# A linear-attention layer and a mixture of experts in one kernel: bo by a product, k turned from its 16-bit halves, x loaded once, another order between attention and experts

## The reference

```
x = x + attention(layernorm(x))
x = x + experts(layernorm(x))

attention: q = elu(x Wq + bq) + 1, k = elu(x Wk + bk) + 1, v = x Wv + bv, 16 heads of 16
           s += k_i v_i^T ; z += k_i ; out_i = (q_i s) / (q_i z + 1e-6)   (causal, per head)
           result = out Wo + bo
experts:   logits = x router_w^T (8 experts); top 2, softmax of the two logits
           y_e = gelu(x w1_e^T + b1_e) w2_e^T + b2_e   (256 -> 512 -> 256)
           out = sum of the two y_e, each times its probability
```

## Time and profile before

| | us |
|---|---|
| median of 3 runs | 1067.27 |
| lowest, highest | 1064.74, 1071.63 |
| the profiled execution | 1070.12 |
| its span, first to last instruction | 1068.0 |

### The profile page before, as it was taken

How to read it: one execution, slowest core, us unless ns; L and a number is a source line. 1 busy time by engine, 2 the same in 40 slices (tenths; PEclk the granted TensorE clock), 3 DMA queues, 4 the chain that set the end, 5 groups by cost and what they waited for, 6 DMA issues and landing times.

```text
span 1068.0 us, 31902 instructions
## 1 busy us (share of the span) xinstructions
PE 941.2 (88%) x10010; PEld 771.1 (72%) x10011; DVE 835.4 (78%) x2220; ACT 657.2 (62%) x1248; POOL 670.5 (63%) x580
## 2 busy tenths in 40 slices
PE   6789889988898898899888925899999999999995
PEld 3467667766776676677667723678999999999994
DVE  5779999999999999999998775456666666666663
ACT  8667776777677767767775332445555555555552
POOL 2226587787778777877878452356656656555665
PEclk9899999999999999999999856999999999999998
DMA  5916956546655664566455282355555565555554
GB/s 156 214 58 169 256 145 169 149 138 172 159 123 157 160 174 117 157 170 144 140 154 141 87 313 73 62 81 84 99 93 90 94 98 87 93 98 90 89 98 49
DMA packets 127242, 138.84 MB, mean 130 GB/s; under 512 B 12400, under 2 KB 120304, under 8 KB 126512
## 3 DMA queue, kind: packets, MB, share of 16 engines
q1 hardware_dynamic: 100288, 101.45, 38.1%
q0 software_dynamic: 25680, 35.01, 17.9%
q10 hardware_dynamic: 1184, 1.18, 0.4%
HBM read 71.08 MB, written 66.53 MB: 129 GB/s over the span
## 4 chain that ended last, share of the span: by engine, by line
PE 42%; DVE 35%; issue 8%; DMA 6%; ACT 3%; POOL 3%; SPq 1%; POOLq 0%; DVEq 0%; ACTq 0%
PE pF L488 9%; DVE ahl L1132 8%; PE pS L488 8%; PE pU L488 7%; PE pA L488 4%; DVE xn L1145 4%; PE pO L488 4%; DMA out<-yt,to_token 3%; DVE xn L1233 2%; PE pO L594 2%; DVE pd L1216 2%; DVE st L1111 2%; DVE w1s L1252 2%; ACT ahl L875 2%; DVE v L1192 2%
## 5 line engine op out<-in xcount | busy, mean ns | idle before, releaser
L1680 POOL DMA_INDIRECT out<-yt,to_token x135 | 218.1, 1615 | 178.5 <-DVE yt L1528 90.8
L875 ACT ACTIVATE ahl<-pS 128x512 f16<-128x512 f32 x240 | 141.0, 599 | 82.5 <-PE pS L573 80.9
L1132 DVE SCALAR_TENSOR_TENSOR ahl<-pS,ahl 128x512 f16<-128x512 f32 x240 | 160.8, 680 | 19.8 <-ACT ahl L875 19.4
L1581 POOL DMA_INDIRECT expert_in<-xn,cur x128 | 129.1, 1009 | 35.1 <-issue 33.4
L570 PE MATMUL pS<-cbs 128*128 128x512 bf16 x240 | 92.8, 387 | 23.8 <-DVE ahl L1132 19.9
L1055 ACT ACTIVATE g<-pS,b1s 128x256 f32<-128x256 f32 (+1 forms) x140 | 57.3, 462 | 87.9 <-PE pS L488 87.9
L1494 DVE TENSOR_TENSOR ghl<-g,ghl 128x1024 f16<-128x1024 f32 (+1 forms) x68 | 83.0, 1220 | 20.9 <-ACT ghl L1080 20.9
L488 PE MATMUL pS<-gT,w1s 128*128 128x256 f16 (+1 forms) x840 | 96.4, 271 | 1.0 <-DVE gT L1489 0.9
L488 PE MATMUL pF<-w2s,ghl 128*128 x816 | 95.1, 273 | 2.0 <-issue 1.1
L1539 POOL TENSOR_TENSOR rs<-ve,cfs 128x4 f32<-128x4 f32 x31 | 32.2, 1040 | 102.3 <-DVE ve L1102 102.3
L488 PE MATMUL pF<-xT,was 128*128 128x512 f16 x384 | 93.0, 379 | 3.1 <-DVE xT L1137 2.5
(11 more groups left out here) (193 smaller groups left out, 2293.0 us busy)
## 6 DMA issues: line engine op xcount, KB each, us to landing
xg<-expert_in SPq DMA_DIRECT2D x64, 260.0 KB, 3.1
qk_parts<-qkhl SPq DMA_DIRECT2D x32, 512.0 KB, 2.9
qst<-qk_parts SPq DMA_DIRECT2D x96, 128.0 KB
kst<-qk_parts SPq DMA_DIRECT2D x48, 256.0 KB
xs<-x SPq DMA_DIRECT2D x16, 512.0 KB, 5.4
xr<-x SPq DMA_DIRECT2D x16, 512.0 KB, 4.9
out<-x SPq DMA_DIRECT2D x16, 512.0 KB, 3.2
expert_in<-pads SPq DMA_DIRECT2D x16, 260.0 KB, 3.9
```

What stands on the lines that cost most here:

```text
L875: nc.scalar.activation(ahl[:, b % 2, 0, n * 4 * C:(n + 1) * 4 * C], score_bank(fr, n)[:], ACT.Relu).then_inc(sc_hi, 1)
L1132: V.scalar_tensor_tensor(ahl[:, b % 2, 1, cols], score_bank(fr, n)[:], 0.0, ahl[:, b % 2, 0, cols], ALU.max, ALU.subtract).then_inc(sc_lo, 1)
L1581: G.indirect_dma_start(xg_dram, bass.IndirectOffsetOnAxis(ap=cur[:, qp, 2 * b + t:2 * b + t + 1], axis=0), xn2[:, qp, b], None).then_inc(s ...
L1680: G.indirect_dma_start(out, bass.IndirectOffsetOnAxis(ap=to_token[:, c % 2, s:s + 1], axis=0), yt[:, c % 2, s], None, compute_op=ALU.add). ...
```

## The change

- **bo.** `add_bo`, `xr` and its load are gone. `boh` holds bo x 16 / 64 in 16 bits, its high half in 64 rows and its low half in 64 rows; a product of a matrix of ones (128 rows) with it opens each `out_project`. The residual reads `xs`, which now has three buffers.
- **k's state.** `k_rows` turns the two 16-bit halves of k (16 transposes, into 16-bit PSUM), `kn_rows` copies both, and the state is three 16-bit products per block against the halves of v.
- **Queue of SP.** k is sent ahead of q's loads in every step. The load of the next x comes behind the store of x1.
- **Routing.** `pd` at L1216 is gone: ACT makes the exponential from the two top logits in four small activations. The last operation of `row_data` and the count become reductions. `ixf` and `pos` lie in PSUM.
- **Order.** The third and fourth `norm2_apply` and the second are moved apart; `w1_high` and `w1_low` come later in the step.
- **Between the parts.** The table is worked out for 128 lanes at once in narrow operations and turned by six transposes. Idle products of PE are put in three places (12, 24 and 8). The padding blocks go out from ACT's queue, 128 rows for seven lists and 256 for the last, and ACT then runs one small Gelu. Step 14's slots are found earlier. Four full tiles (`PRE`) come ahead of the split tiles; where expert 0 has 1024 rows or more after step 14, their loads do not wait for the last step's scatters nor for the padding. `w2_low` is spread.

```diff
+PRE = 4
+LEAD = PRE + SPLIT
...
 (SP)
+                    if c >= 2:
+                        sp.wait_ge(xn_done, 4 * (i - 2) + 4)
+                    sp.wait_ge(ln1_st, 4 * i + 4)
+                    sp.dma_start(xs[:, (c + 1) % XB], x_steps[bass.ds(i + 1, 1)]...).then_inc(x_in, 16)
-                    sp.dma_start(xr[:, par], x_steps[bass.ds(i, 1)]...).then_inc(xr_in, 16)
-                    if lead:
-                        send(0, q_out)
-                        send(1, k_out)
+                    send(0, q_out)
+                    send(1, k_out)
                     for t, sent in enumerate((q_out, k_out)):
-                        if not lead:
-                            send(t, sent)
                         sp.wait_ge(sent, 16 * i + 16)
...
+            sp.wait_ge(ready_set, 2)
+            sp.wait_ge(lists_ready, 1)
+            odd_steps = sp.value_load(ready_i[0:1, 0:1], ...)
+            rows_ready = sp.value_load(ready_i[0:1, 1:2], ...)
             sp.wait_ge(tab, TAB)
...
                 if c == 0:
+                    sp.wait_ge(lists_ready, rows_ready)
+                    sp.wait_ge(pads_out, 16 * (E + 1))
+                    sp.wait_ge(scat_out[0], 128 * STEPS // 2)
+                    sp.wait_ge(scat_out[1], odd_steps)
+                if c == PRE:
+                    sp.wait_ge(scat_out[1], 128 * STEPS // 2)
                     sp.wait_ge(tail_out, 16 * E)
 (PE)
+                    for a in range(2):
+                        for b in (2 * n, 2 * n + 1):
+                            for k in range(KC):
+                                mm = nc.tensor.transpose(k_turned[:, a, c0:c0 + P], qkhl[:, 1, a * KC + k, b * C:(b + 1) * C], ident_half)
...
-                        mm = nc.tensor.matmul(pU[...], kn[:, b, k * P:(k + 1) * P], v[:, sp_, b, ...], start=True, stop=True)
+                        mm = split3(pU[...], lambda a, _: kn[:, a, b, k * P:(k + 1) * P], lambda a, _: vhl[:, sp_, a, b, ...], 1)
...
+                    nc.tensor.matmul(pA[:, D:2 * D], chs[0:2 * BR, H_ONES:H_ONES + P], boh[:], start=True, stop=False)
+                    split3(pA[:, D:2 * D], ..., KC, go_on=True).then_inc(wo_ps, 1)
...
                 if c == STEPS + 1:
                     out_project(r, 3)
+                    idle_products(12)
                     for b in range(B):
                         route_transpose(b)
...
+            idle_products(24)
+            pe.wait_ge(tab, TAB_SUMS)
+            (six transposes: experts_wide twice into pA, to_turn columns 1 and 0 into pA, 2 and 3 into pU)
+            idle_products(8)
             pe.wait_ge(tab, TAB)
 (ACT)
-            nc.scalar.activation(kn[:, 2 * n:2 * n + 2]..., pU[:], ACT.Copy)
+            nc.scalar.activation(kn[:, :, 2 * n:2 * n + 2]..., k_turned, ACT.Copy)
+                def top_probability():
+                    act.wait_ge(rt, RT * q + 2)
+                    for b in range(B):
+                        nc.scalar.activation(one_exp[:, b, 1:2], mx[:, b, 0:1], ACT.Exp, bias=mx[:, b, 1:2], scale=-1.0)
...
             for n in range(2, W2Q):
                 w2_high(n)
+            act.wait_ge(tail_done, 1)
+            for e in range(E):
+                row = act.value_load(tails_i[0:1, e:e + 1], ...)
+                act.dma_start(xg_dram[bass.ds(row, P)], pads[:, 0]).then_inc(tail_out, 16)   (256 rows for the last)
+            act.wait_ge(lists_ready, 1)
+            act.wait_ge(tail_out, 16 * E)
+            act.sem_inc(lists_ready, 1)
+            nc.scalar.activation(warm[:], one_exp[:, 0, 0:1], ACT.Gelu)
 (DVE)
-                    V.scalar_tensor_tensor(pd[:, 0], mx[:, :, 1], 1.0, mx[:, :, 0], ALU.mult, ALU.subtract)
-                    V.tensor_tensor(cnt[:], oh[:, :, 0], oh[:, :, 1], ALU.add).then_inc(cnt_done, 1)
+                        V.tensor_reduce(cnt[:], oh[:].rearrange("p b t e -> p b e t"), AX.X, ALU.add).then_inc(cnt_done, 1)
-                    V.scalar_tensor_tensor(xn2[:, qp, :, PROB2], pd[:, 2], 1.0, one_exp[:, :, 1], ALU.mult, ALU.mult)
+                    V.tensor_reduce(xn2[:, qp, :, PROB2], one_exp[:, :, 1:3], AX.X, ALU.mult)
...
-                        norm2_apply(1)      (was beside norm2_apply(0); now behind score_lo(1, 2))
-                        norm2_apply(3)      (was beside norm2_apply(2); now behind score_lo(2, 0))
-                if fr and c >= 2:
-                    w1_low()                (was ahead of score_lo(2, 0))
                 if nx or left:
                     norm1_stats(i + 1)
+                if fr and c >= 2:
+                    w1_low()
...
+                if c == STEPS + 1:
+                    row_data()
+                    out_lo(r, 3)
+                    router_slots()
+                    residual(r, 2)
...
+            (table: 33 counted operations, most on 8 to 24 columns, the widest on 256, then four copies out of PSUM)
 (POOL)
-                G.tensor_tensor(xr[:, c % 2], xr[:, c % 2], bos[:]..., ALU.add).then_inc(xr_done, 1)
+                if c == STEPS + 1:
+                    scatter(0)
```

More of the change, by code:

```diff
@@ L296, in tiles @@
         def tiles(engine, body, first=-2):
-            for c in range(first, SPLIT):
+            for c in range(first, LEAD):
                 body(0, c)
-            with engine.Fori(0, (FULL - 2) // 2) as j:
-                for c in (SPLIT, SPLIT + 1):
+            with engine.Fori(0, (FULL - PRE - 2) // 2) as j:
+                for c in (LEAD, LEAD + 1):
                     body(j, c)
@@ L487, in split3 @@
                         pe.wait_ge(*low_wait)
-                    mm = nc.tensor.matmul(out, lhs(a, k), rhs(b_, k), start=(t == 0), stop=(t == len(terms) - 1))
+                    mm = nc.tensor.matmul(out, lhs(a, k), rhs(b_, k), start=(t == 0 and not go_on), stop=(t == len(terms) - 1))
                 return mm
@@ L1478, in _ @@
+            count(V.tensor_copy(table[:, 0], pA[0:1, 256:256 + NS]))
+            count(V.tensor_copy(table[:, 1], pA[0:1, 0:NS]))
+            count(V.tensor_copy(settled[:], pU[0:1, 0:2 * P].rearrange("p (a n) -> p a n", a=2)[:, :, 0:FULL]))
+            settle()
             assert done[0] == TAB, done
-            for n in range(W2Q):
-                w2_low(n)
+            w2_low(1)
             def tile(j, c):
@@ L1621, in body @@
                     scatter(1)
-                if fr and c >= 2:
-                    add_bo(i, c)
                 if sc:
```

379 lines of the change are left out of this document (217 added, 162 removed).

## The result

Changed kernel: **1042.45 us** (median of 4, 1041.82 to 1043.18), before 1068.59 beside it; ratio **0.976**, 95% interval 0.972 to 0.979. The forecast was 1012 us: 55 us of gain, of which 26 came. A second comparison, five rounds, gave 1039.24 against 1067.01, ratio 0.974 (0.971 to 0.977).

What follows compares the result with a forecast made beforehand. Attention was taken as bound by DVE first, PE a little behind, the experts by PE alone. Gains of 46 (steps), 8 (between the parts) and 1 (start) gave 55 us, so 1012 us; range 986 to 1046, 8 in 10.

Steps and rivals of the forecast that it cites:

- the one on SP: SP's queue in attention: k sent first lands its last piece 0 to 3 us earlier, costing nothing.
- Rival 4: Attention steps: PE idles 3 us or more at the head, then half clock; step +2.5 us, 1093 us; chance 0.05.
- rival 3: Attention steps: k's round trip binds, pieces 1 to 2 us too late; step 35, 1033 us; chance 0.08.
- The steady step: Attention: step falls from 36.8 to 33.5 us, with DVE busy 30.6 and PE 32.5.
- The routing terms: DVE in attention: L1216 gone (-1.92), L1233 a reduction (-2.02); sum -3.9 us a step.
- PE's sum: PE in attention: bo +0.44, k's state -0.84, k turned 0; -0.4, so 32.5 us, bounds 31.7 to 34.2.
- The count of steps: Attention: fourteen steps (c = 2 to 15) have the period, so 3.3 x 14 = 46 us gained.
- Between the parts: Attention to experts: hidden layer -5.6 us, table load hidden and full tiles first -2.3; sum -8, bounds -3 and -14.
- The start: Step 1: add_bo no longer holds up DVE's q, -2; preparing boh up to 1; sum -1, between +1 and -4.
- 1: DVE in attention: separated norm2_apply blocked by POOL, waits come back; step 35.9, 1045 us; chance 0.17.
- 2: Attention: PE and DVE overlap well; step 32.2, between the parts -14, 987 us; chance 0.15.
- 5: Attention: hand-overs between ACT, DVE and PE take back DVE's gain; step 36.6, 1062 us; chance 0.05.

Runs made afterwards that it cites:

- the first two comparisons: Changed kernel against the kernel before, 1042.45 us, ratio 0.976; changed kernel with q's halves stored and loaded first again, 1028.02 us, ratio 0.965.
- the places: Kernel before with only DVE's changed order (norm2_apply spread over four places, w1's low half behind norm 1's statistics): 1072.98 us, ratio 0.996.
- either part alone: Kernel before with only DVE's changed order, 1072.98 us, ratio 0.996; kernel before with only the changed routing operations, 1069.42 us, ratio 0.993.
- the order put back: Changed kernel with q's halves stored and loaded before k's from c=2 on: 1028.02 us, ratio 0.965; again beside the unedited one (1039.24), 1028.19 us.
- pairs alone: Changed kernel with q's halves first, norm2_apply in pairs again, w1's low half left at its new place: 1027.33 us, ratio 0.963.
- two variants with k first: Apparently the changed kernel with k's turns and state products in float32, 1034.63 us, and with w1raw's load at the step's head, 1038.73 us.
- one with q first: Apparently the changed kernel with q's halves first and w1raw's load at the step's head: 1026.63 us, ratio 0.960.
- both variants with k first: Changed kernel with a useless 512 KB transfer behind k's loads, 1129.36 us; with k's loads held until q's have landed, 1128.19 us.

## Why the prediction was right or wrong

**The step that failed** is the one on SP: "the last piece should land 0 to 3 us earlier; as long as that exceeds what the step loses elsewhere, it costs nothing". k's loads were issued earlier, but q's loads began 2.4 us later and all share the DMA engines, so the last piece landed 0.6 us later on the mean, and 1.9 us later (15.7 us behind k's halves instead of 13.8) in the interval of 35.8 us, which PE waited out. And it was costed at nothing although it made PE's instructions late and put stops into five steps. Together 14 us between the first two comparisons, 11 on one chip. Of the 3.9 us lost in the interval of 35.8, 3.1 go with the order by the first two executions and 1.3 by the two on one chip. Rival 4 had the shape of it (an idle PE, then half clock), but its cause was a wait for k at the head, and it sat in each step; rival 3 put the lateness at 1 to 2 us in steps that have the slack to hide it. No part of the prediction asked what else goes by the DMA engines.

**The steady step** was right: 33.5 forecast, 33.6 measured; DVE 30.6 and 30.3, PE 32.5 and 32.2. Inside, the sizes moved. w1_low, taken at -0.4, gave -0.8 of busy time. The routing terms, taken at -3.9, are -3.5 in DVE's busy time, but by themselves 8.1 us of the kernel, and the places 4.6. The premise that the step follows DVE's busy time does not hold for either part alone (2.6 and 3.5 us off DVE, 0.3 and 1.3 off the step); the sum holds with the rest of the change there, which part of it is needed is not shown, and so it is partly luck. PE's sum (-0.4) came out at -0.7. Two slips in the prediction's working change nothing: its terms give PE a lower bound of 32.2 us, not 31.7, and rival 4 takes off 3.1 us where the forecast's own gain is 3.3.

**The count of steps** was 14, and there are 13: the next interval was already 31.9 us before. With the order put back the 13 gained 37.2 us, not 46: 3.3 for that count, and 5.7 since their mean is 33.9 and not 33.5 us.

**Between the parts**, 7.5 us to the hidden layer instead of 5.6, with 15.7 us from the chain's start where 18 were forecast: the chain took 7.4 us (7.5 forecast), but the padding was issued in 8.4 us instead of 9.7 and had landed 3.2 us later instead of 3.9. The further 2.3 us for full tiles first did not come: from the hidden layer to the end it takes 412.2 to 415.7 us in all executions with the changed experts and 411.7 to 414.4 in those with the old ones. Adds that wait for adds are in the ramp of both; what they cost was not tested.

**The start**, -1 forecast, +1.4 measured: DVE's q is 0.69 us each as forecast, but ACT then waits 6.7 us for w1raw, where it waited 1.8 before. What this costs was not tested. The order has no part in it: up to the first store both orders are the same queue, and executions of the changed kernel's start differ by themselves (77.2 to 79.2 us).

**Rivals.** 1 is refuted: norm2_apply means 0.79, and pairs alone change nothing. 2, 4 and 5 did not come. By the spans, 55 were forecast; less 14.6 with the order (11.5 in the 13 intervals, 3.1 in the next), 4.1 for the 14th step, 5.7 for the mean step, 1.5 between the parts and 2.4 in the start, 26.7 are left, and 27.0 came.

**Open:** It is shown that the order makes the stops: in the changed kernel beside its version with q first on one chip; on another, in two variants with k first and not in one with q first; and in the kernel before once k is sent ahead; and that with it packets of PE's instructions start late by PE's own count, with every stop on these chips just behind the start of one. Not shown is what delays the packets (with q first a useless transfer made no stop), why four as late made none, nor what stops PE on the one chip in each step with k first and in some with q first.

## What to carry to other kernels

In straight-line code with short products, watch for idle time that "issue" ended, and compare the packets of the instruction queue with the engine's count of instructions. A transfer reordered off the critical path can still stop PE, and where PE has no slack a stop near 2 us cost its own length, or up to twice that where half clock followed. An engine's busy time is a poor price for a part of a change: two parts that took 2.6 and 3.5 us off DVE's 34.9 shortened the step by 0.3 and 1.3 when they stood alone. Count the steps that really have the period that you shorten. And compare a variant with more than one execution, on its own chip.

## What the runs showed of the hardware

- With k first PE stopped in mid-group with no releaser, 0.5 to 2.6 us, at the same five products in two executions (7.7 and 7.2 us in the sum), each stop ending 2.5 to 2.9 us behind the start of a 16 KB packet of the instruction queue.
- Behind stops of 1.6, 2.0 and 2.6 us (106.5, 382.7 and 487.8 us) the granted clock was 0.50 for some 3 us, behind one of 2.18 us in the second execution for over 6; behind two there of 1.79 and 1.96 us it stayed at 1.00.
- On one of the chips both variants with k first took 1128 us, 5% over the kernel before, with a product or three each 0.73 us; there PE had 8 and 10 stops of 0.2 to 0.6 us with q first, too.
- A DVE operation of four numbers took 1.39 us in its form with two SBUF inputs and 0.153 as a reduction.
- The load of ACT's table took 1.28 us, in the changed kernel as before, and the next activation began 0.01 us behind it.
